# Weighting an expert's rows on the chip and scattering them with addition into one row per token

## The chip, the core and the metric

The kernel runs on one core of a Trainium2 chip. Five engines work side by side, each with its own list of instructions: TensorE (PE in the profile; PEld is its loading of weights), VectorE (DVE), ScalarE (ACT), GpSimd (POOL) and SyncE (SP), which issues most transfers between the off-chip memory and the on-chip memory. POOL issues the indirect transfers, those whose rows go to addresses out of a table. The engines meet only through semaphores: an instruction waits until a counter has reached a value. The metric is the time of one execution on the device in microseconds (us).

## What is computed

An input of 4096 tokens (16 sequences of 256) of 128 numbers goes through four layers that each add to it: attention a (one head), a routed feed-forward, attention b (16 causal heads), and the routed feed-forward again with the same weights. The change is in the feed-forward:

```python
gates = softmax(x @ router_w)                     # 8 experts
idx1, idx2 = best expert, second best expert      # each with a place in its expert, if below capacity
g1, g2 = gates of the two, 0 where there was no place
g1, g2 = g1 / max(g1 + g2, eps), g2 / max(g1 + g2, eps)
expert_out = silu(expert_in @ w1 + b1) @ w2 + b2  # 1280 places (slots) an expert
y = sum over the token's two slots of g * expert_out
out = y + 0.1 * (silu(x @ sw1 + sb1) @ sw2 + sb2) # the shared expert
```

## The kernel before

`x` stays on chip for all 4096 tokens, as 32 tiles of 128 tokens; four tiles are a quad, and there are eight quads. A routed layer runs in 56 items of 256 rows (`ITEMS`): 10 pieces of the shared expert (`FRONT`), then 40 chunks (`NCH`, five for each expert, `CHUNKS`), then the other 6 pieces. For an item TensorE forms a first product (`first_mm`), ACT applies `Silu` into `hT` (`silus`), TensorE forms the second product (`second_mm`), one item later in its order, and DVE takes the result out of PSUM (`y_copy`). DVE also prepares the operand of the item after (`x_split`) and, once for an expert, splits its weights (`w1_split`).

The expert's rows travel through off-chip memory. POOL's `dispatch` writes each normalised token, with its number behind it, to its two slots in `x_slots` (line 611). SP's `load` brings a chunk of 256 slots back, with the numbers in `x_id`. DVE's `rows_of` works out for each slot the row of `y_rows` to which its result goes: the token's number in the first half for a first choice, 4096 further for a second choice, and a number out of range for an empty slot, which the transfer then leaves out (`row_cur`, line 1828). `y_copy` adds the bias `b2` to the product and writes it to `yo`, a ring of five buffers (line 1845). POOL's `scatter` sends it in two indirect transfers of 128 rows (line 626). Slots number 10240, assignments at most 8192.

When all scatters have landed (`rows_back`), two rows come back for each token. After layer 0 SP's `y_load` brings them by quads into `yab`, and DVE's `combine` multiplies each by its factor `gate` and adds it to `x` (line 1937): quad 0 ahead of attention b, the others in the course of it, between the instructions of `attn_b_pair`. After layer 1 SP loads all into `y_all` (line 485, 16 loads), and the end is divided: for quads 0 to 5 DVE adds the first row with its factor (`tail_half`, line 1911), ACT scales the second (`scale_tail`, line 1337) and DVE adds it (`tail_add`, line 1925); for quads 6 and 7 TensorE multiplies both rows by diagonal matrices that ACT has made out of the factors (lines 1186 and 1331), and DVE adds the sum out of PSUM. SP stores each quad when it is done.

The order of work on each engine is the order in which the code is written: `moe(l, start, upto)` on each engine walks through the items, and the calls of the tail and of `combine` stand in it at fixed items. The factors are worked out in 14 steps of DVE (`gates`), one in each of 14 chunks.

```python
for j in range(CH):
    pool.indirect_dma_start(y_rows, bass.IndirectOffsetOnAxis(ap=row_cur[:, g % ROWS, j:j + 1], axis=0),
                            yo[:, g % RING, j, :], None, bounds_check=last_row, oob_is_err=False
                            ).then_inc(sca[g % RING], 16)
```

Of the kernel before, what the change touches and what calls it, by code (L numbers as in the profile page):

```python
# [15 lines left out]
P = 128  # L16
# [7 lines left out]
CH = 2  # L24
# [13 lines left out]
OUT = 4.0 * T  # L38
# [14 lines left out]
LIMITS, GATES = 7, 14  # L53
# [37 lines left out]
def build(nc, x_in, hd_mask, w_q, w_k, w_v, w_o, attn_W, attn_b, out_W, out_b, router_w,  # L91
          w1, b1, w2, b2, sw1, sb1, sw2, sb2, out):
    with ExitStack() as ctx:
# [7 lines left out]
        y_rows = nc.dram_tensor("y_rows", [2 * T, D], F32).ap()  # L101
# [12 lines left out]
        slot_id = sb("slot_id", [P, SLOT_TILES])  # L114

# [25 lines left out]
        r3 = sb("r3", [P, 4]); t2 = sb("t2", [P, 4, E]); t3 = sb("t3", [P, 4, E]); r4 = sb("r4", [P, 4])  # L141
# [5 lines left out]
        lim1 = sb("lim1", [P, E]); lim2 = sb("lim2", [P, E]); ge1 = sb("ge1", [P, SLOT_TILES]); ge2 = sb("ge2", [P, SLOT_TILES])  # L147
        row_add = sb("row_add", [P, SLOT_TILES])
        zs = sb("zs", [P, NT]); gx = sb("gx", [P, NT, E]); es = sb("es", [P, NT]); den = sb("den", [P, NT])
        gk = sb("gk", [P, 2, NT]); gate = sb("gate", [P, 2, NT])  # L150

        with ExitStack() as shared_place:
            y_all = shared_place.enter_context(nc.sbuf_tensor("y_all", [P, 2, NT, D], F32))
# [9 lines left out]
        with ExitStack() as shared_place:  # L163
# [14 lines left out]
        row_cur = sb("row_cur", [P, ROWS, CH], U32)  # L178

# [75 lines left out]
        S.row_set = sem("row_set")  # L255
# [14 lines left out]
        S.comb = sem("comb")  # L270
        S.y_used = sem("y_used")
        S.tail_scaled = sem("tail_scaled")
        S.diag_set = sem("diag_set")
        S.tail_mm = sem("tail_mm")
        S.tail_half_dve = sem("tail_half_dve")
# [43 lines left out]
        N_CONST_POOL, KEY_MASK_STEPS = 16, SPAN + 8  # L319
# [4 lines left out]
        TAIL_SCALE = {54: (0, 1, 2), 55: (3, 4, 5)}  # L324

        BY_PE = 6
        diag_places = (v_ext[:, :, :, :, :].rearrange("p a k (h i) r -> p (a k h) (i r)", i=4),
                       oT[:, :, :].rearrange("p g (j q) -> p (g j) q", q=P))

        def diag(k):  # L330
            return diag_places[k // 16][:, k % 16, :]


        pe_bank = {6: bank[5], 7: bank[4]}
# [15 lines left out]
        def _(sp):  # L350
# [34 lines left out]
            def load(l, c):  # L385
# [3 lines left out]
                need(sp, S.row_set, g - RING + 1)  # L389
# [24 lines left out]
            y_in = (S.y_in0, S.y_in1)  # L414
# [31 lines left out]
            def attn_b_pair(i):  # L446
                for h in range(2):
                    if valid(i + 3):
                        y_load(i + 3, h)
                    if valid(i + 1):  # L450
                        restack(i + 1, h)
# [1682 lines left out]
```

## Time and profile before

| what | value |
|---|---|
| time, median of 3 runs (lowest, highest) | 770.65 us (766.17, 772.09) |
| the profiled execution: its time, its span | 770.89 us, 769.1 us |
| TensorE busy (share of the span) | 704.7 us (92%) |
| DVE busy | 523.9 us (68%) |
| ACT busy | 449.7 us (58%) |
| POOL busy | 440.9 us (57%) |
| mean granted TensorE clock | 0.977 |

All numbers below are from that one profiled execution. The span reaches from its first to its last instruction; its time is that of the device and is a little longer. A busy share is a mean over stages that are limited by different things, so what a change is worth is read in the stage it touches: which engine has no idle time there, and what the others wait for.

### The profile page before, as it was taken

The page shows a single profiled execution, that of the slowest core. Times are in us where ns is not written, and L with a number is a line of the kernel's source. Part 1 is how long each engine was busy: PE and PEld are TensorE (multiplying, and loading weights), DVE is VectorE, ACT ScalarE, POOL GpSimd, SP SyncE. Part 2 cuts the span into 40 slices and gives each one's busy share as a digit, 9 for nine tenths or more (in the row PEclk, how much of TensorE's full clock was granted, in tenths as well). Part 3 has the DMA queues.
Part 4 walks back from the last instruction along what each step waited for, and adds up shares of the span by engine and source line. Part 5 has one row for each costly group of instructions (what it writes and reads, how often), then busy time and mean ns, then how long its engine had stood idle before and what let it go on. Part 6 is the DMA issues. An engine that isn't in the chain of part 4 may idle for free.

```text
span 769.1 us, 18168 instructions
## 1 busy us (share of the span) xinstructions
PE 704.7 (92%) x6152; PEld 641.6 (83%) x6152; DVE 523.9 (68%) x1665; ACT 449.7 (58%) x1144; POOL 440.9 (57%) x564
## 2 busy tenths in 40 slices
PE   6888789799999997889999998999999899999996
PEld 5777689799999996667777776777779899999996
DVE  5877765366556565768888988877676556655536
ACT  2565454344444443677878878787755444456545
POOL 6367777166666651344545767777777265666640
PEclk9999869999999998899999999999999999999999
DMA  7997111455556334333533434333201346555328
GB/s 245 309 323 183 46 48 55 58 113 108 108 99 133 78 104 118 104 99 109 142 101 91 126 119 147 100 95 111 62 30 53 53 84 131 109 97 112 90 68 287
DMA packets 167715, 89.35 MB, mean 116 GB/s; under 512 B 120576, under 2 KB 151890, under 8 KB 167528
## 3 DMA queue, kind: packets, MB, share of 16 engines
q1 hardware_dynamic: 155704, 69.89, 36.6%
q0 software_dynamic: 9216, 17.34, 6.6%
q10 hardware_dynamic: 2704, 0.98, 0.6%
q8 instruction: 50, 0.82, 0.5%
q14 instruction: 41, 0.34, 0.1%
HBM read 49.63 MB, written 39.67 MB: 116 GB/s over the span
## 4 chain that ended last, share of the span: by engine, by line
PE 57%; DVE 5%; POOL 5%; DMA 5%; SPq 4%; issue 4%; ACT 3%; ACTq 0%; DVEq 0%; POOLq 0%
PE bank L940 22%; PE bank L919 19%; PE bank L1021 4%; DMA qc<-qk_rows 3%; SPq L439 3%; POOL x_slots L611 3%; PE bank L980 2%; PE bank L998 2%; PE bank L1002 2%; POOL pt L695 2%; DVE negp L1951 1%; PE bank L976 1%; PE bank L981 1%; ACT pt L1389 1%; PE bank L1040 1%
## 5 line engine op out<-in xcount | busy, mean ns | idle before, releaser
L1291 ACT ACTIVATE hT<-bank,bias_T 128x256 f32<-128x256 f32 x448 | 175.7, 476 | 186.4 <-PE bank L919 186.3
L626 POOL DMA_INDIRECT y_rows<-yo,row_cur x160 | 158.5, 990 | 127.9 <-DVE yo L1845 103.2
L1951 DVE TENSOR_REDUCE negp<-bank 128x2 f32<-128x512 f32 (+1 forms) x192 | 129.6, 685 | 44.3 <-PE bank L981 27.1
L940 PE MATMUL bank<-w_s,hT 128*128 128x128 f32 x1280 | 155.9, 275 | 0.0
L611 POOL DMA_INDIRECT x_slots<-xr,slot_u x128 | 129.9, 1015 | 38.7 <-issue 35.5
L940 PEld LDWEIGHTS bank<-w_s,hT 128*128 128x128 f32 x1280 | 150.0, 192 | 0.0
L919 PE MATMUL bank<-xT_hl,w_hl 128*128 128x256 f32 x960 | 135.4, 291 | 9.1 <-DVE xT_hl L1719 9.1
L695 POOL TENSOR_SCALAR_AFFINE_SELECT pt<-pt 128x512 f32<-128x512 f32 x128 | 86.0, 680 | 92.7 <-ACT pt L1389 92.2
L1389 ACT ACTIVATE pt<-bank 128x512 f32<-128x512 f32 x192 | 107.8, 596 | 40.3 <-PE bank L1002 38.5
L919 PEld LDWEIGHTS bank<-xT_hl,w_hl 128*128 128x128 f32 x960 | 120.9, 192 | 9.6 <-issue 9.6
L1845 DVE TENSOR_TENSOR yo<-bank,b_b 128x256 f32<-128x256 f32 x80 | 33.9, 424 | 98.7 <-PE bank L940 98.7
L940 PE MATMUL bank<-sw_s,hT 128*128 128x128 f32 x512 | 63.0, 276 | 2.1 <-issue 2.1
L940 PEld LDWEIGHTS bank<-sw_s,hT 128*128 128x128 f32 x512 | 60.2, 193 | 2.8 <-issue 2.8
L1021 PE MATMUL bank<-pt,v_ext 128*32 128x256 f32 (+1 forms) x1024 | 55.5, 335 | 6.6 <-POOL pt L695 6.4
L919 PE MATMUL bank<-xT_hl,sw_hl 128*128 128x256 f32 x384 | 55.5, 296 | 2.1 <-issue 1.5
L919 PEld LDWEIGHTS bank<-xT_hl,sw_hl 128*128 128x128 f32 x384 | 49.8, 198 | 2.9 <-issue 2.1
L1021 PEld LDWEIGHTS bank<-pt,v_ext 128*32 128x32 f32 x1024 | 26.9, 110 | 27.8 <-POOL pt L695 10.4
L980 PE MATMUL bank<-bdk,qc 96*128 96x256 f32 x128 | 48.9, 382 | 1.1 <-DVE negp L1951 0.4
L998 PE MATMUL bank<-qc,bdk 128*128 128x256 f32 x256 | 41.5, 284 | 0.2 <-ACT pt L1389 0.2
L980 PEld LDWEIGHTS bank<-bdk,qc 96*128 96x128 f32 x128 | 25.6, 200 | 17.2 <-issue 8.7
L976 PE MATMUL bank<-bdk,qc 128*128 128x512 f32 x64 | 31.6, 493 | 8.9 <-DMA qc<-qk_rows 8.6
L1002 PE MATMUL bank<-qc,bdk 128*128 128x128 f32 x256 | 37.0, 267 | 2.9 <-ACT pt L1389 2.9
(214 smaller groups left out, 1194.0 us busy)
## 6 DMA issues: line engine op xcount, KB each, us to landing
xg_all<-x_slots SPq DMA_DIRECT2D x316, 32.0 KB
w_s<-in_L_ffn_w SPq DMA_DIRECT2D x32, 256.0 KB
qk_rows<-qks SPq DMA_DIRECT2D x16, 512.0 KB, 3.6
bdk<-qk_rows SPq DMA_DIRECT2D x187, 32.0 KB
qc<-qk_rows SPq DMA_DIRECT2D x45, 128.0 KB, 2.8
x_slots<-xg_all SPq DMA_DIRECT2D x1, 5440.0 KB, 21.7
y_rows<-xg_all SPq DMA_DIRECT2D x1, 4096.0 KB, 14.3
yab<-y_rows SPq DMA_DIRECT2D x16, 256.0 KB, 3.3
```

What stands on the lines that cost most here:

```text
L611: pool.indirect_dma_start(x_slots, bass.IndirectOffsetOnAxis(ap=slot_u[:, c, t:t + 1], axis=0), xr[:, t, :], None, bounds_check=last_slot, ...
L626: pool.indirect_dma_start(y_rows, bass.IndirectOffsetOnAxis(ap=row_cur[:, g % ROWS, j:j + 1], axis=0), yo[:, g % RING, j, :], None, bounds ...
L695: a = pool.affine_select(out=blk, in_=blk, compare_op=ALU.is_ge, fill=0.0, base=0, pattern=[[0, 4], [1, P]], channel_multiplier=-1)
L919: m = pe.matmul(bk[:, (f % 2) * 256:(f % 2) * 256 + 256], wt[:, wp, f * P:(f + 1) * P], xT_hl[:, w % 2, xp, :], start=(p == 0), stop=(p == 2))
L940: m = pe.matmul(yb(w, l)[:, j * P:(j + 1) * P], hT[:, w % 2, f, j * P:(j + 1) * P], wt[:, f, :], start=(f == 0), stop=(f == FT - 1))
L980: pe.matmul(halves[:, :, 0:P], q[0:96], heads[0:96, :, 0:P], start=True, stop=True)
L998: m = pe.matmul(bk[:, j * SEQ:j * SEQ + SEQ], bdk[:, par, g, 2 * k + j, 0:P], qc[:, par, g, :], start=True, stop=True)
L1002: m = pe.matmul(bk[:, j * P:j * P + P], bdk[:, par, g, j, P:SEQ], qc[:, par, g, P:SEQ], start=True, stop=True)
L1021: m = pe.matmul(OB[32 * j:32 * j + 32, c0 + kt * P:c0 + SEQ], v_ext[:, par, kt, 4 * g + j, :], rhs, start=(kt == 0 and g % 2 == 0), stop=( ...
L1291: a = act.activation(hT[:, w % 2, f, :], HB[2 * (w % 2) + f // 2][:, (f % 2) * 256:(f % 2) * 256 + 256], ACT.Silu, bias=bias_T[:, b0 + f:b ...
L1389: act.activation(pt[:, g % 2, k, :], CB[(g + k) % 2][:, :], ACT.Exp).then_inc(S.exp_done, 1)
L1951: dve.tensor_reduce(dst, AB[(g + k) % 2][:, :].rearrange("p (j k) -> p j k", j=heads), AX.X, ALU.max, negate=True).then_inc(S.amax_done, 1)
```

## The change

The products of an expert are weighted before they leave the chip, and the scatter adds them into one row for each token. The weight of a slot (`share`) is 1 for a token's first choice and, for its second choice, the ratio of the two gates; that ratio now travels with the token in the next column of `xr` (column `D + 1`), where `second` writes it. `y_copy` forms `share * product + share * b2`, and ACT makes `share * b2` ahead of it (`b2_scaled`, two copies with a factor in each chunk). Empty slots get a weight too, but go to rows behind the tokens' rows (`slot_dump`), one for each slot; no row is left out any more. Since both rows of a token go to one address, a chunk that begins an expert waits on POOL until all scatters before it have landed. The layers have a region each in `y_rows`, so the second layer waits no longer for the first one's reading.

One row comes back for each token, with one factor (`gate`, now 11 steps). `combine` is called once for a quad (in attention b at the later of the two former places), `y_load` once. In the end DVE adds quads 0, 1, 2, 3, 5 and 7 with their factor (`tail`), and ACT scales quads 4 and 6, which DVE then adds. TensorE's products with diagonals and ACT's diagonals are gone. The last piece of the shared expert is added to `x` last.

```diff
-LIMITS, GATES = 7, 14
+LIMITS, GATES = 7, 11
...
-        y_rows = nc.dram_tensor("y_rows", [2 * T, D], F32).ap()
+        y_rows = nc.dram_tensor("y_rows", [LAYERS * T + E * CAP, D], F32).ap()
...
-        TAIL_SCALE = {54: (0, 1, 2), 55: (3, 4, 5)}
-
-        BY_PE = 6
...
+        BY_ACT = {54: 4, 55: 6}
...
-            def y_load(p, c):
-                need(sp, (S.comb, S.y_used)[c], p)
-                rows = y_rows[c * T + QUAD * p:c * T + QUAD * (p + 1), :].rearrange("(q t) d -> q t d", q=P)
-                sp.dma_start(yab[:, c, :, :], rows).then_inc(y_in[c], 16)
+            def y_load(p):
+                need(sp, S.y_used, p - 1)
+                rows = y_rows[QUAD * p:QUAD * (p + 1), :].rearrange("(q t) d -> q t d", q=P)
+                sp.dma_start(yab[:, p % 2, :, :], rows).then_inc((S.y_in0, S.y_in1)[p % 2], 16)
...
             def scatter(l, c):
                 g = NCH * l + c
                 pool.wait_ge(S.yo_ready, item_of_chunk(l, c) + 1)
-                pool.wait_ge(S.row_set, g + 1)
-                if c == 0:
-                    if l == 0:
-
-                        pool.wait_ge(S.bdk_zeroed, 16)
-                    else:
-                        pool.wait_ge(S.y_used, PAIRS)
+                pool.wait_ge(S.share_set, g + 1)
+                if g == 0:
+                    pool.wait_ge(S.bdk_zeroed, 16)
+                if g > 0 and c % CHUNKS == 0:
+
+                    for r in range(RING):
+                        pool.wait_ge(sca[r], 32 * (g // RING))
                 for j in range(CH):
                     pool.indirect_dma_start(y_rows, bass.IndirectOffsetOnAxis(ap=row_cur[:, g % ROWS, j:j + 1], axis=0),
-                                            yo[:, g % RING, j, :], None, bounds_check=last_row, oob_is_err=False
+                                            yo[:, g % RING, j, :], None, bounds_check=last_row, oob_is_err=True, compute_op=ALU.add
                                             ).then_inc(sca[g % RING], 16)
...
+            def b2_scaled(l, c):
+
+                g = NCH * l + c
+                act.wait_ge(S.share_set, g + 1)
+                if c >= 2:
+                    act.wait_ge(S.yo_ready, item_of_chunk(l, c - 2) + 1)
+                elif l > 0:
+                    act.wait_ge(S.yo_ready, item_of_chunk(l - 1, NCH - 2 + c) + 1)
+                for j in range(CH):
+                    a = act.activation(b2_share[:, c % 2, j, :], b2_b[:, c // CHUNKS, :], ACT.Copy, scale=share[:, g % ROWS, j:j + 1])
+                a.then_inc(S.b2_shared, 1)
...
-                dve.tensor_tensor(row_cur[:, g % ROWS, :], x_id[:, g % RING, :, 0], row_add[:, CH * c:CH * c + CH], ALU.add
-                                  ).then_inc(S.row_set, 1)
+                dve.scalar_tensor_tensor(out=row_cur[:, g % ROWS, :], in0=x_id[:, g % RING, :, 0], scalar=float(l * T),
+                                         in1=row_add[:, CH * c:CH * c + CH], op0=ALU.add, op1=ALU.max)
+                need(dve, S.yo_ready, item_of_chunk(*divmod(g - ROWS, NCH)) + 1 if g >= ROWS else 0)
+                dve.tensor_tensor(share[:, g % ROWS, :], x_id[:, g % RING, :, 1], is_first[:, CH * c:CH * c + CH], ALU.max
+                                  ).then_inc(S.share_set, 1)
...
-                e = c // CHUNKS
-                dve.tensor_tensor(yo[:, g % RING, :, :], rows, b2_b[:, e:e + 1, :].broadcast_to([P, CH, D]), ALU.add
-                                  ).then_inc(S.yo_ready, 1)
+                dve.wait_ge(S.b2_shared, g + 1)
+                for j in range(CH):
+                    a = dve.scalar_tensor_tensor(out=yo[:, g % RING, j, :], in0=rows[:, j, :], scalar=share[:, g % ROWS, j:j + 1],
+                                                 in1=b2_share[:, c % 2, j, :], op0=ALU.mult, op1=ALU.add)
+                a.then_inc(S.yo_ready, 1)
...
+            def tail(q):
+                dve.wait_ge(y_back[q], 16)
+                dve.wait_ge(S.gated, GATES * LAYERS)
...
+                for t in range(4 * q, 4 * q + 4):
+                    a = dve.scalar_tensor_tensor(out=x[:, t, :], in0=y_all[:, t, :], scalar=gate[:, t:t + 1],
+                                                 in1=x[:, t, :], op0=ALU.mult, op1=ALU.add)
...
-                        if h == 0 and g in (1, 3) and valid(i + 2):
-                            combine(i + 2, g // 2)
+                        if h == 0 and g == 3 and valid(i + 2):
+                            combine(i + 2)
```

Two places of DVE's order show what moves. The first is a chunk in the middle of a routed layer; `bank` is the PSUM tile with the second product, `b_b` is `b2_b` and `b_share` is `b2_share`, and the words in brackets are the semaphores that an instruction waits for. Before:

```order
L1714 STREAM_TRANSPOSE x_cols<-xg_all 128x256 [waits loaded3,h_done]
L1717 CAST xT_hl<-x_cols 128x256 [waits xg_used]
L1719 TENSOR_TENSOR xT_hl<-x_cols,xT_hl 128x256 [waits xT_hi]
L1828 TENSOR_TENSOR row_cur<-xg_all,row_add 128x2 [waits loaded3]
L1845 TENSOR_TENSOR yo<-bank,b_b 128x256 [waits scattered1,yo_done]
```

The same chunk in the changed kernel:

```order
L1685 STREAM_TRANSPOSE x_cols<-xg_all 128x256 [waits loaded3,h_done]
L1688 CAST xT_hl<-x_cols 128x256 [waits xg_used]
L1690 TENSOR_TENSOR xT_hl<-x_cols,xT_hl 128x256 [waits xT_hi]
L1799 SCALAR_TENSOR_TENSOR row_cur<-xg_all,row_add 128x2 [waits loaded3]
L1802 TENSOR_TENSOR share<-xg_all,is_first 128x2
L1822 SCALAR_TENSOR_TENSOR yo<-bank,share,b_share 128x128 [waits b2_shared,scattered1,yo_done]
L1822 SCALAR_TENSOR_TENSOR yo<-bank,share,b_share 128x128
```

One small instruction is added behind `row_cur`, and the addition of the bias has become two instructions that also wait for ACT's `b2_share`.

The second place is the end of DVE's list; `x<-bank,x` at lines 1838 and 1814 is the copy of a last piece of the shared expert, and `y_back5` counts the loads of quad 5. Before, from the addition of quad 3 on:

```order
L1925 TENSOR_TENSOR x<-x,y_all 128x512 [waits tail_scaled,tail_half_dve]
L1911 SCALAR_TENSOR_TENSOR x<-y_all,gate,x 128x128 [waits yo_ready,y_back5]
L1911 SCALAR_TENSOR_TENSOR x<-y_all,gate,x 128x128 x3
L1925 TENSOR_TENSOR x<-x,y_all 128x512 [waits tail_scaled,tail_half_dve]
L1838 SCALAR_TENSOR_TENSOR x<-bank,x 128x256 [waits bias_added,yo_done]
L1925 TENSOR_TENSOR x<-x,y_all 128x512 [waits tail_scaled,tail_half_dve]
L1925 TENSOR_TENSOR x<-x,bank 128x512 [waits tail_mm,yo_ready] x2
```

And in the changed kernel, from the addition of quad 4 on:

```order
L1897 TENSOR_TENSOR x<-x,y_all 128x512 [waits tail_scaled,yo_ready]
L1814 SCALAR_TENSOR_TENSOR x<-bank,x 128x256 [waits bias_added,yo_done]
L1889 SCALAR_TENSOR_TENSOR x<-y_all,gate,x 128x128 [waits yo_ready,gated,y_back5]
L1889 SCALAR_TENSOR_TENSOR x<-y_all,gate,x 128x128 x3
L1889 SCALAR_TENSOR_TENSOR x<-y_all,gate,x 128x128 [waits yo_ready,gated,y_back7]
L1889 SCALAR_TENSOR_TENSOR x<-y_all,gate,x 128x128 x3
L1897 TENSOR_TENSOR x<-x,y_all 128x512 [waits tail_scaled,yo_ready]
L1814 SCALAR_TENSOR_TENSOR x<-bank,x 128x256 [waits tail_last,bias_added,yo_done]
```

Six whole-quad additions are gone from DVE's tail, the copy of the last piece stands at its very end, and quad 0 has moved one item forward, to just behind the copy of item 52.

## Rows read from the trace of the kernel before

**Rows 1.** By stage: length; busy us (instructions) of each engine; granted clock; DMA share, GB/s.
```profile
172.00:280.00 108.00, 108.00 (x942) 108.00 (x942) 61.96 (x189) 53.19 (x136) 66.79 (x70) 1.00 0.50 103
306.00:570.00 264.00, 242.60 (x2360) 192.09 (x2361) 212.87 (x549) 200.18 (x489) 158.11 (x227) 0.98 0.35 104
746.00:769.10 23.10, 17.20 (x150) 16.84 (x148) 14.47 (x41) 13.14 (x40) 0.00 (x0) 0.96 0.84 274
```
**Rows 2.** Timeline of one chunk: start, us, instruction, idle before and its end.
```profile
261.22 0.97 POOL L626 DMA_INDIRECT y_rows<-yo,row_cur  x1 [0.97 <-DVE yo L1845]
...
261.95 1.57 ACT L1291 ACTIVATE hT<-bank,bias_T 128x256 f32<-128x256 f32 x4 [1.65 <-PE bank L919]
...
262.50 0.97 POOL L626 DMA_INDIRECT y_rows<-yo,row_cur  x1 [0.30 <-issue]
...
263.74 0.42 DVE L1845 TENSOR_TENSOR yo<-bank,b_b 128x256 f32<-128x256 f32 x1 [1.59 <-PE bank L940]
...
264.44 0.97 POOL L626 DMA_INDIRECT y_rows<-yo,row_cur  x1 [0.97 <-DVE yo L1845]
```
**Rows 3.** Timeline of the tail, the same columns.
```profile
743.54 0.97 POOL L626 DMA_INDIRECT y_rows<-yo,row_cur  x1 [0.30 <-issue]
...
746.15 8.23 SPq L485 DMA_DIRECT2D y_all<-y_rows  x16
...
751.21 0.42 DVE L1838 SCALAR_TENSOR_TENSOR x<-bank,x 128x256 f32<-128x256 f32 x1 [2.13 <-PE bank L940]
...
752.21 2.18 DVE L1911 SCALAR_TENSOR_TENSOR x<-y_all,gate,x 128x128 f32<-128x128 f32 x8
...
757.64 0.42 DVE L1838 SCALAR_TENSOR_TENSOR x<-bank,x 128x256 f32<-128x256 f32 x1 [0.42 <-PE bank L940]
...
759.24 2.02 PE L940 MATMUL bank<-sw_s,hT 128*128 128x128 f32 x16 [1.64 <-issue]
...
760.23 1.13 DVE L1911 SCALAR_TENSOR_TENSOR x<-y_all,gate,x 128x128 f32<-128x128 f32 x4
...
761.28 0.68 DVE L1925 TENSOR_TENSOR x<-x,y_all 128x512 f32<-128x512 f32 x1
...
764.47 1.27 DVE L1925 TENSOR_TENSOR x<-x,bank 128x512 f32<-128x512 f32 x2
```
**Rows 4.** Groups by line: shapes, count; busy us, mean ns; idle before.
```profile
L1694 DVE SCALAR_TENSOR_TENSOR x<-bank,rsum,x 128x128 f32<-128x128 f32 x32 | 9.6, 341 | 2.2 <-PE bank L812 2.2
...
L1337 ACT ACTIVATE y_all<-y_all,gate 128x128 f32<-128x128 f32 x24 | 7.2, 402 | 0.0
...
L1828 DVE TENSOR_TENSOR row_cur<-xg_all,row_add 128x2 uint32<-128x2 f32 x80 | 12.2, 153 | 0.0
```
**Rows 5.** Instructions that write `y_rows`: the scatters, ns minimum/median/maximum, first and last start.
```profile
L626 POOL DMA_INDIRECT y_rows<-yo,row_cur x160: 970/972/1167, 151.7 to 743.5; - x160
```
**Rows 6.** Timeline at the end of layer 0, the columns of rows 2.
```profile
278.60 0.97 POOL L626 DMA_INDIRECT y_rows<-yo,row_cur  x1 [0.30 <-issue]
...
280.91 12.95 SPq L419 DMA_DIRECT2D yab<-y_rows  x5
...
284.10 2.38 DVE L1937 SCALAR_TENSOR_TENSOR x<-yab,gate,x 128x128 f32<-128x128 f32 x8
...
288.17 1.04 POOL L568 TENSOR_TENSOR rstd<-ve,neg_half 128x4 f32<-128x4 f32 x1
...
290.34 1.10 DVE L1499 TENSOR_SCALAR xn<-x,mv,rstd 128x128 f32<-128x128 f32 x4
```
**Rows 7.** Line 611, the dispatch's indirect transfers (128): time from issue to landing.
```profile
DMA to landing us min/median/max: 2.3/2.4/6.1
```
**Rows 8.** Waits of TensorE for DVE, 306 to 570 us: total, times, longest.
```profile
PE bank L988 <- DVE sel L1595: 1.8, 3, 0.6
...
PE bank L976 <- DVE negp L1951: 0.2, 1, 0.2
```
**Rows 9.** Line 485, the 16 loads of `y_all`: time from issue to landing.
```profile
DMA to landing us min/median/max: 2.7/5.3/7.7
```

More of the change, by code:

```diff
@@ L475, in _ @@
             for p in range(2):
-                for c in range(2):
-                    y_load(p, c)
+                y_load(p)
             for i in range(-1, PAIRS + 1):
@@ L482, in _ @@
             for q in range(PAIRS):
-                for c in range(2):
-                    rows = y_rows[c * T + QUAD * q:c * T + QUAD * (q + 1), :].rearrange("(p t) d -> p t d", p=P)
-                    sp.dma_start(y_all[:, c, 4 * q:4 * q + 4, :], rows).then_inc(y_back[q], 16)
+                rows = y_rows[T + QUAD * q:T + QUAD * (q + 1), :].rearrange("(p t) d -> p t d", p=P)
+                sp.dma_start(y_all[:, 4 * q:4 * q + 4, :], rows).then_inc(y_back[q], 16)
             for q in range(PAIRS):
-                sp.wait_ge(S.tail_dve, q + 1)
+                if q < PAIRS - 1:
+                    sp.wait_ge(S.tail_dve, q + 1)
+                else:
+                    sp.wait_ge(S.yo_ready, ITEMS * LAYERS)
                 sp.dma_start(out_rows[:, 4 * q:4 * q + 4, :], x[:, 4 * q:4 * q + 4, :]).then_inc(S.stored, 16)
@@ L1634, in limits @@
                     if l == 1:
-                        dve.wait_ge(S.row_set, NCH)
-                    dve.scalar_tensor_tensor(out=row_add[:, :], in0=ge1[:, :], scalar=T + OUT, in1=ge2[:, :],
-                                             op0=ALU.mult, op1=ALU.add).then_inc(S.limits, 1)
+                        dve.wait_ge(S.share_set, NCH)
+                    dve.scalar_tensor_tensor(out=row_add[:, :], in0=live[:, :], scalar=0.5, in1=slot_dump[:, :],
+                                             op0=ALU.is_lt, op1=ALU.mult).then_inc(S.limits, 1)
             def gates(l, k):
@@ L1872, in moe @@
                     if l == 1 and w == ITEMS - 2:
-                        tail_half(0)
-                        tail_half(1)
+                        tail(1)
+                    if l == 1 and w == ITEMS - 1:
+                        tail_add(4)
                     if l == 0 and w == ITEMS - 3:
-                        combine(0, 0)
-                        combine(0, 1)
+                        combine(0)
                         stats_b(0)
@@ L1935, in combine, with tail_add @@
+            def tail_add(q):
+                dve.wait_ge(S.yo_ready, quad_pieces(1, q))
+                dve.wait_ge(S.tail_scaled, tuple(BY_ACT.values()).index(q) + 1)
+                xs = x[:, 4 * q:4 * q + 4, :]
+                dve.tensor_tensor(xs, xs, y_all[:, 4 * q:4 * q + 4, :], ALU.add).then_inc(S.tail_dve, 1)
+            def combine(q):
+                dve.wait_ge((S.y_in0, S.y_in1)[q % 2], 16 * (q // 2 + 1))
+                dve.wait_ge(S.yo_ready, quad_pieces(0, q))
                 for j in range(4):
@@ L2106, in _ @@
             moe(1, START, ITEMS)
-            tail_half(5)
-            tail_add(4)
+            tail(5)
+            tail(PAIRS - 1)
+            tail_add(6)
             y_copy(1, ITEMS - 1)
-            for q in range(5, PAIRS):
-                tail_add(q)
 _INS = ['L0_attn_a_x', 'L0_attn_a_head_dim_mask', 'L0_attn_a_w_q', 'L0_attn_a_w_k', 'L0_attn_a_w_v', 'L0_attn_a_w_o',
```

159 lines of the change are left out of this document (54 added, 105 removed).

## Prediction, made before the changed kernel ran

> **What bounds the kernel now.** I read first the table by stage [rows 1]: in the routed feed-forward stretches (172 to 280 us and, alike, 645 to 746) TensorE is busy for the whole stretch, 108.00 of 108.00 us, while DVE has 61.96, ACT 53.19 and POOL 66.79. One item (256 rows: first product, second product) lasts 3.22 us there, read from the start of one chunk's first scatter to the next, 261.22 to 264.44 [rows 2]. In such an item POOL issues two scatters 1.28 us apart and then waits 0.97 us for DVE's rows; DVE waits 1.59 us for TensorE before it writes `yo`; ACT waits 1.65 us before its `Silu`. So work added to DVE, ACT or POOL in a chunk is free up to about these three numbers, and work taken from them there brings nothing. Attention b (306 to 570 us) has TensorE busy 242.60 of 264 us. The last 23.1 us are another regime: TensorE has 17.20 busy, POOL nothing. There DVE runs almost without a gap from 751.21 us on and finishes the last two quads of `x` at 764.47 + 1.27 = 765.74 us [rows 3]; the span ends at 769.1, 3.36 us later, with the last store.
>
> **What the change costs in a chunk (80 of them).** DVE: the addition of the bias, one instruction with 1.59 us of idle time ahead of it, becomes two `scalar_tensor_tensor` on 128x128 out of PSUM. The same form takes 341 ns at line 1694 [rows 4], so 0.68 us in place of 0.42. `rows_of` gets a second instruction like its first, 153 ns [rows 4]. Together +0.41 us against 1.59 us idle. In the chunks where `w1_split` falls too, `x_split` still stands ahead of it, so TensorE's next operand isn't late. ACT: two scaled copies of 128x128, 402 ns each at line 1337 [rows 4], 0.80 us against 1.65 idle [rows 2]. They stand behind the `Silu` of their item; what they wait for (`share_set`, and `yo_ready` of two chunks earlier) is an item old. I cost both at nothing; if the cover were gone, 0.4 us by 80 chunks is 32 us. The gate computation loses three of its fourteen steps, hidden in the same way.
>
> **POOL, where the change is decided.** A scatter now adds. Each still is one indirect transfer of 128 rows, which takes POOL 972 ns in the median [rows 5]. At each fifth chunk POOL must now wait until all scatters before it have landed. A plain scatter lands about 2.3 us after its start: the last of layer 0 starts at 278.60 and SyncE reads its rows at 280.91 [rows 6]; the sister scatter at line 611 has 2.4 us as its median and 6.1 at most [rows 7]. An expert's five chunks last 5 x 3.22 = 16.10 us. Ten issues put the last one's start at 9 x 1.28 = 11.52 us, and its landing at 11.52 + 2.3 = 13.8. That leaves 2.3 us in each expert before the new wait delays the next one. With an issue longer by dT and a landing longer by dL, the overrun of an expert is 9 dT + dL - 2.3.
>
> No row shows an adding scatter. The bounds from rows: at the low end dT = dL = 0 (a gain is excluded: the same 128 rows are sent, and none is now left out). At the high end each costs what two plain ones do, dT = 0.97 and dL = 2.3, since an addition reads the row and writes it: an overrun of 8.7 us for each of seven boundaries and 9 x 0.97 + 2.3 = 11.0 in the last expert, 72 us in a layer and about 140 in both. I take dT = 0 and dL up to 2, hence nothing, by the nearest row: the 160 scatters vary from 0.97 to 1.17 us only [rows 5], although their rows fill 10240 slots with 8192 assignments, so about a fifth of the rows are left out today, unevenly. The issue time doesn't follow the work sent.
>
> The Trainium skill has two rules on this. The page "Collectives: The Full Stack", section "Stop ④ — SDMA + CCE: where bytes move and the add happens", says that an addition in the DMA engine takes two reads and one write, that is a second read descriptor for each row. "DMA: Bandwidth & Descriptors", section "Anatomy of one DMA — SWDGE (gpsimd) path", says that many descriptors can be emitted before their cost shows. By the second rule the sum below stands; by the first, if issue goes with descriptors, rival A does. No run here shows either yet.
>
> **The end of layer 0.** Rows are asked for at 280.91, `combine` starts at 284.10, its rstd is done at 288.17 + 1.04 = 289.21 and used at 290.34 [rows 6], behind a copy that waits for TensorE. That is 1.13 us of slack; one quad of four instructions less before the statistics (1.05 us, from 760.23 to 761.28 [rows 3]) makes it 2.2. So no gain here, and 2.2 us of cover for late rows.
>
> **Attention b.** DVE loses four instructions of 128x128 in each of six pairs, 24 x 0.34 = 8 us, but TensorE waited for DVE's work 2.6 us in all there, four entries from 1.8 down to 0.2 [rows 8]. Bounds 0 to 2.6; I take 0.4, because the removed instructions are not the ones waited for.
>
> **The tail, where the gain is.** Loads: eight of 256 KB, not sixteen; no path ends there. I lay DVE's new order along the old times [rows 3]. The copy of item 52 starts at 751.21, and with the operand split behind it takes 1.00 us (to 752.21); quad 0, now between the two, 1.05: 753.26. Quad 1: 754.31. Copy 53, 0.42: 754.73. Quads 2 and 3: 756.83. Addition of quad 4, scaled by ACT, half of 1.27: 757.46. Copy 54 waits for TensorE until 757.64 as before, to 758.06. Quads 5 and 7: 760.16. Addition of quad 6: 760.79. Copy of item 55: 761.21. Before, the same point was 765.74: a gain of 4.5 us. TensorE's final product ran from 759.24 to 761.26, held up by twelve scalings on ACT that are four now; if it stayed there, the copy ends at 761.7 and the gain is 4.0. The sixteen products with diagonals lie in the shade of DVE and bring nothing of their own. Quad 0 must be there at 751.55: asked for at 746.15, landing 2.7 us at the least, 5.3 in the median of sixteen queued ones [rows 3, 9]. The first in the queue takes the least, so about 748.9: 2.7 us of cover. The stores follow as before, 3.36 us behind.
>
> **Sum.** 0 (chunks) - 0 (layer 0) - 0.4 - 4.5 = -4.9 us against the profiled execution's own 770.89 us (span 769.1 and 1.8 around it): 766.0 us. The median of the three runs is 770.65, the same to 0.03%. TensorE's granted clock stays what it is in the stages, 1.00 [rows 1]; nothing is moved on it.
>
> **The rivals.**
> A, slower: the adding scatter takes POOL longer to issue. It decides from dT of about 0.15 us with dL = 1 (9 x 0.15 + 1 = 2.3). At dT = 0.25, dL = 1 an expert overruns by 0.95: 7 x 0.95 + 9 x 0.25 + 1 = 9.9 us late per layer, less the covers 2.2 and 2.7: 14.9 in all, 766.0 + 14.9 = 781 us; at the double issue about 905. For it: POOL has only 0.97 us left in an item [rows 2]. Against: the issue time that doesn't vary. [...]
> B: the issue is the same, but each landing costs a second round trip, dL = 2.3 to 4. At 4 (a landing of 6.3, near the 6.1 of [rows 7]) the overrun is 1.7, 7 x 1.7 + 4 = 15.9 late per layer, less covers 26.9: 793. At 2.3 there is no overrun, only 2.3 late: 766. In the middle, 3: 7 x 0.7 + 3 = 7.9 late, 10.9 after covers: 777.
> C: DVE's relief in attention b is worth all 2.6 us, not 0.4: 763.8. For it: the removed work is three times that. Against: it stands where TensorE isn't waiting.
> D: the change doesn't bring its gain: quad 0's rows come after 751.55, DVE waits there, and the tail keeps its length: 769.5. Against: 2.7 us of cover.
>
> **How the numbers follow.** Forecast 0.52, A 0.22, B 0.14, C 0.06, D 0.06. The predicted time is the forecast's, 766.0; its own range is 763.5 to 768. The range given reaches from 761 to 800: it leaves out the heavier half of A (0.11) and the little below 761, and takes in B and D. About 1% is what a measurement of this kernel can tell from no change, that is 763 to 778.4 us. Faster than that needs C and a tail better than laid out: 0.07. Slower is nearly all of A and a part of B: 0.25. Within: 0.68.
>
> **What would show it.** Right: scatters on POOL of 0.97 us again; waits for landing below 2 us at each fifth chunk and gone two chunks later; 3.22 us an item; DVE's last copy at about 761 and the end some 4.6 us earlier. Wrong: scatters over 1.1 us, POOL with no idle time in the feed-forward, `y_all` loads asked for later than 748, DVE idle before quad 0, or ACT's scaled copies ahead of a late `Silu`.

## The result, and the profile after

The changed kernel takes 845.57 us in the median of four runs (844.02 to 848.18), beside 770.08 us for the kernel before (four runs, 766.17 to 772.09). The ratio is 1.097, with a 95% interval of 1.093 to 1.102: slower by a tenth, where 766.0 us was predicted, in a range of 761 to 800. The profiled execution has a span of 846.3 us, against 769.1 before.

The first place to look is the one on which the prediction said the change is decided, the scatters. All instructions of their line in the changed kernel, with their minimum, median and maximum in ns, and the time from issue to landing of the same line:

```profile
L616 POOL DMA_INDIRECT y_rows<-yo,row_cur x160: 1541/1549/1902, 152.3 to 825.3; - x160
...
DMA to landing us min/median/max: 3.2/3.3/6.0
```

Before, the same 160 transfers took 970/972/1167 ns [rows 5]. Adding makes each 0.577 us longer on POOL in the median, and the shortest one with adding (1541 ns) is longer than the longest one before (1167 ns). A landing comes 3.3 us after its start, 0.9 to 1.0 later than the 2.3 to 2.4 that the prediction had for a plain one [rows 6, 7] (and 0.6 later than the median of the plain ones in the first experiment below).

The stages of the changed kernel (length; busy us and instructions of PE, PEld, DVE, ACT, POOL; granted clock; DMA share, GB/s):

```profile
172.00:280.00 108.00, 95.84 (x772) 95.08 (x771) 60.34 (x217) 59.71 (x166) 78.57 (x50) 0.94 0.70 93
306.00:570.00 264.00, 227.98 (x2139) 184.48 (x2137) 188.00 (x487) 183.34 (x453) 148.99 (x214) 0.95 0.34 103
700.00:800.00 100.00, 85.46 (x681) 84.09 (x680) 52.01 (x181) 52.82 (x148) 73.37 (x48) 0.93 0.64 82
```

TensorE had 108.00 of 108 us and 942 instructions in the first stretch [rows 1]; now it has 95.84 and 772. It no longer sets the pace. The timeline of POOL at the end of one expert and the start of the next shows what does (start, us, instruction, idle time before it and what ended it):

```profile
210.42 1.56 POOL L616 DMA_INDIRECT y_rows<-yo,row_cur  x1 [0.31 <-DMA y_rows<-yo,row_cur]
212.28 1.55 POOL L616 DMA_INDIRECT y_rows<-yo,row_cur  x1 [0.30 <-DVE yo L1822]
214.14 1.55 POOL L616 DMA_INDIRECT y_rows<-yo,row_cur  x1 [0.30 <-issue]
218.22 1.55 POOL L616 DMA_INDIRECT y_rows<-yo,row_cur  x1 [2.54 <-DMA y_rows<-yo,row_cur]
220.08 1.55 POOL L616 DMA_INDIRECT y_rows<-yo,row_cur  x1 [0.30 <-DVE share L1802]
```

Inside an expert POOL starts a scatter every 1.855 us, 0.30 us after the one before has ended: the 0.97 us in which it waited for DVE's rows once in each item [rows 2] are gone. Two scatters take 3.71 us, an item of TensorE 3.22. At the boundary it then waits for the landing: from 214.14 to 218.22 us, 4.08 us from start to start instead of 1.855. Over the 14 boundaries these gaps are 3.93 to 6.74 us, 4.50 in the mean.

How POOL's lateness comes to TensorE stands in the table of waits of the changed kernel (who waited for whom: us in total, times, longest):

```profile
DVE yo L1822 <- issue: 38.8, 14, 5.9
PE bank L909 <- DVE xT_hl L1690: 36.6, 14, 4.9
```

`yo` is a ring of five buffers. When POOL is behind, `y_copy` finds no free buffer, and the `x_split` of the item after, which stands behind `y_copy` on DVE, comes late to TensorE's first product. The first row is put down to "issue", but the timeline shows the ring. This is the last chunk of layer 1, and the second scatter of the chunk five places earlier, which used the same buffer:

```profile
804.68 1.55 POOL L616 DMA_INDIRECT y_rows<-yo,row_cur  x1 [0.30 <-issue]
...
807.92 0.61 DVE L1822 SCALAR_TENSOR_TENSOR yo<-bank,share,b_share 128x128 f32<-128x128 f32 x2 [2.27 <-DMA y_rows<-yo,row_cur]
```

`y_copy` starts 3.24 us after that scatter, which is a time to landing, and in no chunk does it start sooner than this. The two rows of the table are the clearest path and not the whole loss: in the whole run TensorE is idle for 120.6 us in place of 64.4, and busy for 725.7 us in place of 704.7, with 32 instructions fewer, at a granted clock of 0.939 in place of 0.977.

The lateness can be followed through the run by the first and last scatter of each layer, read from the timelines:

| | before | changed | difference |
|---|---|---|---|
| layer 0, first to last scatter | 151.74 to 278.60: 126.86 | 152.34 to 319.68: 167.34 | +40.5 |
| last of layer 0 to first of layer 1 | to 615.00: 336.40 | to 659.88: 340.20 | +3.8 |
| layer 1, first to last scatter | to 743.54: 128.54 | to 825.26: 165.38 | +36.8 |
| last scatter to the end of the span | to 769.1: 25.6 | to 846.3: 21.0 | -4.5 |

Two layers of nearly 40 us each are nearly the whole loss, the part after the last scatter is shorter, and a small loss of 3.8 us stands in between.

### The profile page after: what moved, and what is told of

The parts are those of the page before. It is cut to its first block, busy times and chain, and to the rows that moved or that the text cites. A ratio compares the mean times of both kernels' runs of the same rounds, so it can differ in the third digit from the quotient of the medians.

```text
span 846.3 us, 18422 instructions
## 1 busy us (share of the span) xinstructions
PE 725.7 (86%) x6120; PEld 660.3 (78%) x6120; DVE 526.0 (62%) x1777; ACT 487.5 (58%) x1272; POOL 533.7 (63%) x565
## 3 DMA queue, kind: packets, MB, share of 16 engines
q0 software_dynamic: 27136, 19.42, 16.0%
HBM read 45.44 MB, written 39.67 MB: 101 GB/s over the span
## 4 chain that ended last, share of the span: by engine, by line
PE 51%; issue 9%; POOL 9%; DVE 7%; DMA 4%; ACT 3%; SPq 3%; DVEq 0%; ACTq 0%; POOLq 0%
PE bank L930 19%; PE bank L909 16%; PE bank L1011 4%; POOL y_rows L616 4%; POOL x_slots L601 2%; SPq L427 2%; PE bank L970 2%; PE bank L988 2%; DMA qc<-qk_rows 2%; PE bank L992 2%; POOL pt L685 2%; DVE negp L1918 1%; PE bank L1030 1%; PE bank L971 1%; DMA y_rows<-yo,row_cur 1%
## 5 line engine op out<-in xcount | busy, mean ns | idle before, releaser
L616 POOL DMA_INDIRECT y_rows<-yo,row_cur x160 | 250.7, 1567 | 115.4 <-DVE yo L1822 54.6
L909 PE MATMUL bank<-xT_hl,w_hl 128*128 128x256 f32 x960 | 143.1, 302 | 36.6 <-DVE xT_hl L1690 36.6
L930 PE MATMUL bank<-w_s,hT 128*128 128x128 f32 x1280 | 162.7, 282 | 0.0
L909 PEld LDWEIGHTS bank<-xT_hl,w_hl 128*128 128x128 f32 x960 | 127.5, 202 | 39.2 <-DVE xT_hl L1690 31.6
L930 PEld LDWEIGHTS bank<-w_s,hT 128*128 128x128 f32 x1280 | 157.5, 200 | 0.0
L1822 DVE SCALAR_TENSOR_TENSOR yo<-bank,share,b_share 128x128 f32<-128x128 f32 x160 | 48.7, 346 | 130.0 <-PE bank L930 82.0
L930 PE MATMUL bank<-sw_s,hT 128*128 128x128 f32 x512 | 66.5, 287 | 0.3 <-issue 0.3
L1310 ACT ACTIVATE b_share<-b_b,share 128x128 f32<-128x128 f32 x160 | 56.3, 412 | 15.2 <-DVE yo L1822 15.1
L930 PEld LDWEIGHTS bank<-sw_s,hT 128*128 128x128 f32 x512 | 64.3, 204 | 0.5 <-issue 0.4
L1814 DVE SCALAR_TENSOR_TENSOR x<-bank,x 128x256 f32<-128x256 f32 x32 | 13.5, 422 | 41.8 <-PE bank L930 41.5
```

Of the source, the lines that this page charges most:

```text
L909: m = pe.matmul(bk[:, (f % 2) * 256:(f % 2) * 256 + 256], wt[:, wp, f * P:(f + 1) * P], xT_hl[:, w % 2, xp, :], start=(p == 0), stop=(p == 2))
L930: m = pe.matmul(yb(w, l)[:, j * P:(j + 1) * P], hT[:, w % 2, f, j * P:(j + 1) * P], wt[:, f, :], start=(f == 0), stop=(f == FT - 1))
L1310: a = act.activation(b2_share[:, c % 2, j, :], b2_b[:, c // CHUNKS, :], ACT.Copy, scale=share[:, g % ROWS, j:j + 1])
```

## The experiments

Times are medians of four to ten runs; the run of eight forms was taken once. The kernel before, run beside them, took 769.93 us beside the two experiments with the longer POOL instruction, and 769.59 beside the others.

**Everything but the adding.**

```diff
-                                            yo[:, g % RING, j, :], None, bounds_check=last_row, oob_is_err=True, compute_op=ALU.add
+                                            yo[:, g % RING, j, :], None, bounds_check=last_row, oob_is_err=True
```

> The changed kernel with a plain scatter in place of the adding one; all else stays, the wait at each expert's first chunk, the rows for empty slots and the new tail included. A token's later row overwrites its earlier one, so the second of its two experts is lost from the sum. Theory (the time that POOL takes to issue an adding scatter, and its landing, are the whole loss): POOL's scatters take 0.97 us again, an item lasts 3.22 us, the wait at an expert's first chunk costs TensorE nothing, and the rest of the prediction holds: 766 us (764 to 769). Rival 1 (the loss is in what goes with it: ACT's scaled biases, two instructions more on DVE, no row left out of a scatter any more): 780 to 845 us. Rival 2 (the loss is adding, but the tail brings nothing): 769 to 772 us.

Measured: 765.43 us, ratio to before 0.994 (0.991 to 0.997). Scatters and stage of this run:

```profile
L616 POOL DMA_INDIRECT y_rows<-yo,row_cur x160: 969/975/1220, 152.6 to 744.8; - x160
...
172.00:280.00 108.00, 106.83 (x929) 106.67 (x928) 69.47 (x250) 70.37 (x196) 67.26 (x68) 1.00 0.52 111
```

The whole loss of 80 us is in one word of one line, the addition. What goes with it (the scaled biases on ACT, the longer `y_copy`, the rows of empty slots, the wait itself) costs next to nothing as long as the scatter is plain: TensorE lacks 1.2 us of 108 in this stretch. Both rivals of this experiment fall.

The wait is there all the same. At each of the 14 boundaries POOL stands idle for 2.04 to 4.28 us, 41 us in all, and starts a scatter 3.02 to 5.25 us after the one before (3.9 in the mean); the plain scatters of this run land after 2.7 us in the median, 2.2 to 4.5. One boundary in POOL's timeline:

```profile
184.24 0.97 POOL L616 DMA_INDIRECT y_rows<-yo,row_cur  x1 [0.31 <-issue]
188.66 0.97 POOL L616 DMA_INDIRECT y_rows<-yo,row_cur  x1 [3.45 <-DMA y_rows<-yo,row_cur]
```

POOL stays in step over an expert all the same, because two plain scatters take it 2.56 us of an item of 3.22 and it makes up 0.66 us in each. The tail of this run is the one that the prediction laid out (timeline, columns as above):

```profile
752.22 1.13 DVE L1889 SCALAR_TENSOR_TENSOR x<-y_all,gate,x 128x128 f32<-128x128 f32 x4
...
758.32 0.42 DVE L1814 SCALAR_TENSOR_TENSOR x<-bank,x 128x256 f32<-128x256 f32 x1
758.66 2.18 DVE L1889 SCALAR_TENSOR_TENSOR x<-y_all,gate,x 128x128 f32<-128x128 f32 x8
760.76 0.69 DVE L1897 TENSOR_TENSOR x<-x,y_all 128x512 f32<-128x512 f32 x1
761.36 0.42 DVE L1814 SCALAR_TENSOR_TENSOR x<-bank,x 128x256 f32<-128x256 f32 x1
```

The last copy ends at 761.78 us; the prediction had 761.21, or 761.7, and before it was 765.74 [rows 3].

**Adding, without the wait.**

```diff
-                if g > 0 and c % CHUNKS == 0:
-                    for r in range(RING):
-                        pool.wait_ge(sca[r], 32 * (g // RING))
...
-    ... in0=live[:, :], scalar=0.5, in1=slot_dump[:, :],
+    ... in0=live[:, :], scalar=8.0, in1=slot_dump[:, :],
```

> The changed kernel, still adding, but every slot's row goes to a row of its own behind the tokens' rows, and the wait at each expert's first chunk is gone; what comes back for the tokens are zeros, so the routed feed-forward is lost from the output. This leaves the longer issue alone. Theory (two parts: longer issue, and the wait for landing at 14 boundaries): POOL is busy without a pause, 2 x 1.855 = 3.71 us an item against 3.22, 40 x 0.49 = 19.6 late in a layer, less covers of 2.2 and 2.7, plus about 1 for each landing: 766 + 36 = 802 us (797 to 808); the rest to 845.6 is the wait. Rival 1 (the wait makes nearly all of it, since the extra 0.58 us for each transfer would fit into POOL's pauses): 766 to 775 us. Rival 2 (the wait costs nothing of its own, adding to rows in use is what is slow): above 830 us.

Measured: 807.87 us, ratio 1.049 (1.044 to 1.054). POOL's timeline has no pause any more; two rows of it, and all scatters:

```profile
L612 POOL DMA_INDIRECT y_rows<-yo,row_cur x160: 1542/1550/2066, 149.7 to 784.7; - x160
...
240.31 1.55 POOL L612 DMA_INDIRECT y_rows<-yo,row_cur  x1 [0.30 <-issue]
242.16 1.55 POOL L612 DMA_INDIRECT y_rows<-yo,row_cur  x1 [0.30 <-issue]
```

From the first to the last scatter of layer 0 it is 149.72 to 298.27, 148.55 us, and 40 x 3.71 is 148.4; in layer 1 it is 147.84. So POOL alone sets the pace of both layers. The two parts of the theory are both there, of about the same size: 807.9 - 765.4 = 42 us for the longer issue, 845.6 - 807.9 = 38 us for the wait. The time is 6 us above the 802 expected, at the upper end of the range. Of these, 2 lie between the last scatter of layer 0 and the first of layer 1 (298.27 to 636.84, 338.6 us, against 336.4 before); I had counted on the covers of 2.2 and 2.7 us there and at the end, which the prediction worked out for a TensorE that arrives on time.

**POOL kept busy, without adding.** The run above with plain scatters and, behind each, an instruction of POOL that writes a scratch tile:

```diff
-                                            yo[:, g % RING, j, :], None, bounds_check=last_row, oob_is_err=True, compute_op=ALU.add
+                                            yo[:, g % RING, j, :], None, bounds_check=last_row, oob_is_err=True
                                             ).then_inc(sca[g % RING], 16)
+                    need(pool, S.idle_set, CH * g + j)
+                    pool.iota(idle_pool[:, j, :], [[1, IDLE]], base=0, channel_multiplier=0, allow_small_or_imprecise_dtypes=True
+                              ).then_inc(S.idle_set, 1)
```

> The run before this one (rows of their own, no wait at the boundaries, the routed feed-forward lost from the output) with a plain scatter, and a POOL instruction of some 0.57 us that writes a scratch tile behind each scatter. Theory (it is POOL's own time that delays, whatever it is spent on): the same time as with adding scatters, within 1%, about 802 us. Rival (the DMA engines' additional read or the later landing delays, and POOL's time counts little): 764 to 772 us.

Measured: 765.16 us, ratio 0.994 (0.991 to 0.997). This would be the rival's number, but the added instruction was too short, as POOL's timeline shows:

```profile
229.94 0.99 POOL L615 DMA_INDIRECT y_rows<-yo,row_cur  x1 [0.60 <-DVE yo L1824]
230.94 0.22 POOL L619 IOTA idle_pool<- 128x80 f32 x1
231.33 1.00 POOL L615 DMA_INDIRECT y_rows<-yo,row_cur  x1 [0.17 <-issue]
```

The instruction took 0.22 us, not 0.57, and POOL started a scatter 1.39 us after the one before. Twice that is 2.78 us, which fits into an item of 3.22; POOL still waited 0.6 us for DVE. So the run doesn't decide between the two, but it shows one side of the threshold: 0.11 us more POOL time for each scatter is free, as the prediction's 0.97 us of idle time in an item [rows 2] says.

**POOL kept busy for longer.** The same with 106 numbers in a pattern of two dimensions:

```diff
-                    pool.iota(idle_pool[:, j, :], [[1, IDLE]], ...
+                    pool.iota(idle_pool[:, j, :], [[CH * P, IDLE // CH], [P, CH]], ...
```

> Again plain scatters to rows of their own without the wait at the boundaries (the routed feed-forward is lost from the output), with a longer POOL instruction behind each. The one before was meant to take 0.57 us and took 0.22, so that POOL started a scatter every 1.39 us and both fitted into an item; a pattern like that of the slot numbers, which took 0.54 us for 80 numbers, should take about 0.68 us with 106 and give the 1.86 us of the adding scatters. Theory (POOL's own time delays, whatever it is spent on): the last scatter of layer 0 starts some 20 us later than in the kernel before, near 298, and the time is that of the adding scatters without wait, 807.9 us, within 1% (800 to 812). Rival (the DMA engines' part of adding delays): 764 to 772 us.

Measured: 816.16 us, ratio 1.059 (1.053 to 1.065). POOL's timeline:

```profile
202.21 0.99 POOL L615 DMA_INDIRECT y_rows<-yo,row_cur  x1 [0.18 <-issue]
203.22 0.71 POOL L619 IOTA idle_pool<- 128x106 f32 x1
204.12 0.99 POOL L615 DMA_INDIRECT y_rows<-yo,row_cur  x1 [0.18 <-issue]
```

Now a scatter starts every 1.915 us, 0.06 more than with adding. For 160 scatters that is 9.6 us; less these, the run is at 806.6 us, and the adding scatters without wait took 807.9. (The 816 lie outside the 800 to 812 that I gave, by this excess of POOL time.) POOL's time is what delays, whatever it is spent on. The single runs reach from 809.77 to 817.97 us here and from 806.38 to 809.17 with adding, so the agreement holds to some 4 us, not to 1. Within that, what the DMA engines do more when they add shows no cost of its own, although POOL's queue takes 16.6% of the sixteen engines' time in the page of the adding run and 7.1% in the page of this one.

**All but the adding: plain scatter, busy POOL and the wait.** The first experiment with the same long instruction behind each scatter.

```diff
                                             yo[:, g % RING, j, :], None, bounds_check=last_row, oob_is_err=True
                                             ).then_inc(sca[g % RING], 16)
+                    need(pool, S.idle_set, CH * g + j)
+                    pool.iota(idle_pool[:, j, :], [[CH * P, IDLE // CH], [P, CH]], base=0, channel_multiplier=0, allow_small_or_imprecise_dtypes=True
+                              ).then_inc(S.idle_set, 1)
```

> The plain scatter to the tokens' rows with the wait at each expert's first chunk, and the same long POOL instruction behind each scatter (a token's later row overwrites its earlier one). This has all of the changed kernel but the adding itself. Theory (POOL's time and the wait for landing make the loss; a plain scatter lands 2.4 us after its start, an adding one 3.3): 845.6 less 14 x 0.9 = 833 us (825 to 848). Rival 1 (the wait is long because adding to rows lands late under load): nearer to the run without wait, 805 to 818 us. Rival 2 (POOL's time counts little, see the other run): 764 to 775 us.

Measured: 837.27 us, ratio 1.088 (1.083 to 1.094); 833 was expected. (The nearness is in part luck: the expectation didn't count the instruction's excess of 9.6 us, without which the run is at 827.7, still within the 825 to 848 given.) A boundary in layer 1 (POOL's timeline):

```profile
693.34 1.00 POOL L619 DMA_INDIRECT y_rows<-yo,row_cur  x1 [0.18 <-issue]
694.36 0.73 POOL L623 IOTA idle_pool<- 128x106 f32 x1
696.51 1.04 POOL L619 DMA_INDIRECT y_rows<-yo,row_cur  x1 [1.43 <-DVE yo L1828]
```

From start to start it is 3.17 us here (3.04 to 5.61 over the 14, mean 3.53), against 4.50 in the mean with adding. POOL goes on 0.7 to 0.8 us after a landing, as the two runs that show landings say: with adding the shortest and longest gaps, 3.93 and 6.74 us, go with landings of 3.2 and 6.0, and in the first experiment 3.02 and 5.25 go with 2.2 and 4.5. The gaps carry the sums: with adding 14 x (4.50 - 1.855) = 37 us, and 845.6 - 807.9 = 37.7 were measured; plain 14 x (3.53 - 1.915) = 22.6, and 837.3 - 816.2 = 21.1 were measured. So some 21 us of the wait are there for a plain scatter too once POOL has no slack, and about 15 more come from the later landing of the adding one. (Whether it lands later because it adds, or because it adds to rows that were written shortly before, no run separates.)

**What sets the time of an issue.** Eight forms in one kernel.

```diff
+                    at = lambda n: bass.IndirectOffsetOnAxis(ap=row_cur[0:n, g % ROWS, j:j + 1], axis=0)
+                    k = c % 8
+                    if k == 0:
+                        pool.indirect_dma_start(y_rows, at(P), src, None, ...
+                    elif k == 1:
+                        pool.indirect_dma_start(y_rows, at(64), src[0:64], None, ...
+                    elif k == 2:
+                        pool.indirect_dma_start(half_rows, at(P), src[:, 0:64], None, ...
+                    elif k == 3:
+                        pool.indirect_dma_start(y_rows, at(32), src[0:32], None, ...
...
```

> Eight forms of the scatter in one kernel, chunk by chunk: 128 rows of 128 numbers, 64 rows, 128 rows of 64 numbers, 32 rows; first plain, then adding. Rows go to places of their own, without the wait at the boundaries, and a part of the rows is not sent at all, so the routed feed-forward is lost from the output. It is read for the time of one issue on POOL and for its landing; its total says nothing. Theory (POOL's time goes with the descriptors that it writes, one more for each row that adds): adding 64 rows takes what plain 128 rows take or less, the surcharge of 0.58 us at 128 rows falls to about 0.29 at 64 and 0.15 at 32 rows, and rows of half the width change nothing. Rival 1 (a fixed surcharge for each adding instruction): 0.58 us at 32 rows too. Rival 2 (it goes with bytes): the half width has half the surcharge.

Measured, in the order of the forms (128 rows, 64 rows, 128 rows of half the width, 32 rows; first the four plain ones; ns minimum/median/maximum):

```profile
L618 POOL DMA_INDIRECT y_rows<-yo,row_cur x20: 971/1018/1427, 153.1 to 724.4; - x20
...
L620 POOL DMA_INDIRECT y_rows<-yo,row_cur x20: 910/919/926, 156.3 to 727.0; - x20
...
L622 POOL DMA_INDIRECT y_rows<-yo,row_cur x20: 975/978/1137, 159.5 to 729.6; - x20
...
L624 POOL DMA_INDIRECT y_rows<-yo,row_cur x20: 872/882/1017, 162.7 to 732.1; - x20
...
L626 POOL DMA_INDIRECT y_rows<-yo,row_cur x20: 1554/1570/1757, 165.9 to 735.8; - x20
...
L628 POOL DMA_INDIRECT y_rows<-yo,row_cur x20: 1409/1430/1658, 169.7 to 739.5; - x20
...
L630 POOL DMA_INDIRECT y_rows<-yo,row_cur x20: 1554/1562/2076, 173.2 to 743.0; - x20
...
L632 POOL DMA_INDIRECT y_rows<-yo,row_cur x20: 1330/1342/1857, 177.2 to 746.5; - x20
```

Going by the minima, adding costs 0.583 us at 128 rows, 0.499 at 64, 0.458 at 32 and 0.579 at half the width. From 128 rows down to 32 the surcharge falls by 0.125 us, 1.3 ns a row; extended to no rows it is still about 0.42. My theory, a surcharge that halves with the rows, falls. Rival 1 is nearly right: some 0.42 us belong to the instruction, 0.17 at 128 rows to the rows, nothing that can be seen to the bytes. So fewer or narrower rows in a transfer would not have saved the change: an adding transfer of 32 rows, 1342 ns, still takes POOL longer than a plain one of 128, 1018.

## Why the prediction was wrong, point by point

- **The step that failed** is "I take dT = 0 ... The issue time doesn't follow the work sent". dT is 0.577 us. The row from which it was taken [rows 5] was read too far: it shows that one kind of transfer takes the same time on POOL, with rows left out or not. It says nothing about another kind. The last experiment shows both to be true: the rows hardly matter (1 ns each for a plain one, from 872 ns at 32 to 971 at 128), the kind of the instruction does. The bounds (0 to 0.97) held the value; the choice between them was what failed, although the text itself had worked out that 0.15 us decides.
- **A second step was off: "That leaves 2.3 us in each expert".** It ends the wait at the landing, and takes the landing at 2.3 us. In the run without adding a boundary takes 3.9 us from start to start in the mean, so 16.10 - 11.52 - 3.9 = 0.7 us were left. The sign "waits for landing below 2 us ... and gone two chunks later" is missed there too (2.04 to 4.28 us; in the expert that begins at 188.66 us POOL doesn't catch up before its end). It cost little in that run, and with adding it is part of what the formula lacks, in the next point.
- **Rival A**, with its place, its mechanism and its direction, is what happened; its price was set at dT = 0.25, and the real surcharge is more than twice that. The formula was right in kind: with dT = 0.577 and dL = 0.9 an expert overruns by 9 x 0.577 + 0.9 - 2.3 = 3.8, and the last expert begins 7 x 3.8 = 26.6 us late. For its last scatter the formula adds 9 dT = 5.2, counted from 11.52; but in the kernel before that scatter starts 4 x 3.22 + 1.28 = 14.16 us after the expert's first one, and now 9 x 1.855 = 16.70, so only 2.5 are added: 29.1 us late. Measured are 40.5 and 36.8. Missing are 1.6 and 1.1 us for each boundary. Nearly all of it is the gap, 4.50 us in the mean where the formula has 2.3 + 0.9 = 3.2: the 0.7 us from the landing to the next scatter, a term that the formula doesn't have, and landings later than the median (the gap of 6.74 us is the first one of layer 0).
- **Which rule of the Trainium skill bore on it.** The page "Collectives: The Full Stack", section "Stop ④ — SDMA + CCE: where bytes move and the add happens", by which an addition takes a second read, pointed to A and was weighed too low. That POOL's time goes with the descriptors was the prediction's own "if". The trace has more packets: POOL's queue has 27136 in place of 9216, 112 more for each of 160 scatters. A second read as such can't be seen in its counts, for the queue's bytes (19.42 MB) and the bytes read from off-chip memory (45.44 MB) are the same as in the run without adding. And the time doesn't go with the packets: in the run of eight forms an adding transfer of 32 rows has 16 packets more than a plain one and already costs 0.46 us more, one of 128 rows has 112 more and costs 0.58. (The packets of each form are worked out, not counted: that run's queue has 14976 in all, and less 128 transfers of the dispatch at 32 this fits 20 for each form times 4 x 32 + 144 + 80 + 144 + 48, that is rows + 16 for an adding transfer and 32 for a plain one.)
- **Rival B** was a part: the landing is 0.6 to 1.0 us later. It is counted from the start of the issue, so the 0.577 us by which the issue is longer may be most of it; no run shows this. Its share is the 15 us between the waits with and without adding.
- **The chunks on DVE and ACT, costed at nothing:** right. Without the adding TensorE has 106.83 of 108 us, and with a little POOL work and no wait the time is 765.2. `y_copy`'s pair takes 0.61 us and the added small instruction 153 ns, against 0.68 and 153 laid out.
- **The end of layer 0 and attention b:** the relief of 0.4 us is too small to be told here. From last scatter to first it is 336.06 us in the run without adding (280.84 to 616.90) against 336.40, and 335.12 in the run with the shorter POOL instruction, which has the same attention b. The 2.2 us of cover were no cover for a lateness of 40: in the changed kernel TensorE comes to attention b and waits for the rows. Its timeline behind the last scatter of layer 0:

```profile
319.68 1.55 POOL L616 DMA_INDIRECT y_rows<-yo,row_cur  x1 [0.30 <-issue]
...
325.62 1.14 DVE L1904 SCALAR_TENSOR_TENSOR x<-yab,gate,x 128x128 f32<-128x128 f32 x4 [17.09 <-DMA yab<-y_rows]
...
330.80 0.66 PE L1021 MATMUL bank<-ident,xn 128*128 128x128 f32 x2 [15.16 <-DVE xn L1478]
```

  TensorE stands idle for 15.16 us. Much of this comes back, because it has by then done pieces of the shared expert that the kernel before does in this stretch (2790 of its instructions lie between the two scatters, 2899 before), so that the stretch is only 3.8 us longer. The granted clock is low around this wait (columns as in the stages above; the changed kernel, then the kernel before):

```profile
320.00:340.00 20.00, 8.05 (x31) 7.03 (x32) 6.22 (x23) 2.72 (x7) 6.73 (x15) 0.51 0.29 78
...
340.00:360.00 20.00, 14.79 (x77) 12.32 (x77) 12.69 (x31) 9.13 (x23) 3.16 (x6) 0.84 0.47 142
```

```profile
280.00:300.00 20.00, 18.60 (x153) 17.74 (x151) 13.97 (x38) 7.51 (x19) 5.13 (x13) 1.00 0.33 104
...
300.00:320.00 20.00, 14.81 (x78) 11.31 (x77) 14.04 (x35) 10.17 (x24) 3.53 (x7) 0.74 0.56 164
```

  At 0.51 TensorE runs at its lower level of 1.2 GHz nearly throughout. The kernel before loses clock here too, 20 us later and less. How much of the 3.8 us is the clock wasn't tried.
- **The tail:** right. Without adding, the last copy ends at 761.78 instead of 765.74, 4.0 us earlier, where 4.0 to 4.5 were laid out. The gain is real and is about a twentieth of the loss. (In the changed kernel the last scatter is followed by 21.0 us instead of 25.6, but that is no measure of it: TensorE waits for 13.86 us there, until 833.28, because DVE waits for the rows. The 769.5 of rival D is a slip: without the gain the sum is 770.89 - 0.4 = 770.5.)
- **"TensorE's granted clock stays what it is":** wrong as a consequence of the first point: 0.94 in the stretch from 172 to 280 us where it was 1.00, and 0.939 in the mean against 0.977.

No version here is much faster than the kernel before. What the rest of the change brings is measured by the first experiment, 0.6%, and that run has lost a summand of each token. The changed kernel adds in all 160 transfers; whether fewer would do wasn't tried. Two rows with plain scatters are the kernel before.

## What to carry to other kernels

An instruction that gets a new mode is a new instruction: a row that shows how little the old one varies with its load is no price for the new one, and where a small surcharge decides by the formula, the choice belongs on the cautious side or the forecast in the middle. An engine with low overall use (POOL had 57%) can still be the next bound in one stage: what counts is its idle time in one item, here 0.97 us for two transfers, 0.48 each. A wait for landing costs next to nothing while the engine that waits can make it up (41 us of POOL's idle time in the first experiment, 1.2 us of 108 on TensorE) and nearly its full length once it can't; count it from the start of the last transfer to the start of the next one, not to the landing.

## What the runs showed of the hardware

- An indirect transfer that adds takes POOL 0.58 us longer than one that writes, for 128 rows (1549 against 972 ns); at 32 rows it is still 0.46 us, and the width of a row (512 or 256 bytes) makes no difference (0.583 and 0.579 us). Why the instruction itself costs more stays open.
- It goes out in more packets, 112 more for each transfer of 128 rows at the same bytes, and the share of POOL's queue rises from 7.3% of the sixteen engines' time in the first experiment to 16.0% in the changed kernel. No cost of this in time could be seen, to some 4 us.
- A wait of POOL for its own transfer costs, from start to start, 3.0 us at the least for a plain transfer and 3.9 for an adding one, 0.7 to 0.8 us more than the shortest times to landing in the same runs, 2.2 and 3.2.
- Two POOL instructions that write 80 numbers a partition took 0.22 and 0.54 us: the one with a pattern of one dimension, the other with two.
